# A graph layer with routed experts: a fifth buffer of messages and one-hot matrices, in room taken from the scratch of GpSimd's transfer descriptors

## The reference, cut to what matters

```
x = x + (segment_sum(layernorm(x)[src] * edge_weight, dst) @ W.T + b)
h = layernorm(x)
logits = h @ gate_w + gate_b;  idx = argmax(logits);  prb = softmax(logits)[idx]
pos = rank of the node in the queue of its expert;  kept = pos < capacity
y = (relu(h @ w1[idx] + b1[idx]) @ w2[idx] + b2[idx]) * prb * kept
x = x + y
```

## Time and profile before

| | us |
|---|---|
| median of 3 launches | 2920.89 (2913.4 to 2922.91) |
| the profiled launch, its own time | 2914.76 |
| its span, first to last instruction | 2912.8 |
| mean granted TensorE clock | 0.809 |

### The profile page before, as it was taken

How to read it: one execution, slowest core, us unless ns; L and a number is a source line. 1 busy time by engine, 2 the same in 40 slices (tenths; PEclk the granted TensorE clock), 3 DMA queues, 4 the chain that set the end, 5 groups by cost and what they waited for, 6 DMA issues and landing times.

```text
span 2912.8 us, 33576 instructions
## 1 busy us (share of the span) xinstructions
PE 1961.2 (67%) x9784; PEld 1260.8 (43%) x9784; DVE 1083.5 (37%) x5802; ACT 1086.4 (37%) x2562; POOL 1783.0 (61%) x1868
## 2 busy tenths in 40 slices
PE   2333355456888767777777777777777787785199
PEld 1111133234555544444444444444444454454088
DVE  7766233333444333333333333333343343333032
ACT  6666122223444433333333333333343343332033
POOL 6666666666666666666666666656666666655611
PEclk9999955667888887777777777778888888887599
DMA  6664333344434533443343444435444444433246
GB/s 218 192 202 152 94 94 100 100 131 130 152 116 150 161 118 96 131 145 108 100 143 109 130 126 126 130 94 163 131 131 133 128 130 158 161 118 129 88 158 234
DMA packets 139628, 394.12 MB, mean 135 GB/s; under 512 B 36117, under 2 KB 62741, under 8 KB 128806
## 3 DMA queue, kind: packets, MB, share of 16 engines
q0 software_dynamic: 89472, 243.63, 28.3%
q1 hardware_dynamic: 46276, 135.53, 13.4%
q10 hardware_dynamic: 3698, 12.80, 1.1%
HBM read 496.09 MB, written 40.76 MB: 184 GB/s over the span
## 4 chain that ended last, share of the span: by engine, by line
PE 33%; another core or an unknown queue 30%; DVE 13%; ACT 13%; issue 9%; DVEq 0%; DMA 0%; ACTq 0%; SPq 0%; POOL 0%; POOLq 0%
PE ps L1010 10%; PE ps L980 6%; PE ps L898 5%; PE ps L907 3%; PE ps L998 2%; ACT hmid L815 2%; PE ps L989 2%; ACT L791 2%; PE ps L938 2%; ACT L736 1%; ACT msg L770 1%; DVE aggT L1223 1%; ACT pairs L777 1%; ACT hmid L809 1%
## 5 line engine op out<-in xcount | busy, mean ns | idle before, releaser
L655 POOL DMA_INDIRECT msg<-normed,src_sb x1457 | 1387.7, 952 | 799.6 <-issue 389.8
L1010 PE MATMUL ps<-wsl,hmid 128*128 128x256 f32 x1680 | 488.0, 455 | 165.7 <-ACT hmid L815 123.3
L1223 DVE TENSOR_TENSOR aggT<-aggT,ps 128x192 f32 x293 | 103.9, 354 | 1315.1 <-remote 651.2
L1010 PEld LDWEIGHTS ps<-wsl,hmid 128*128 128x128 f32 x1680 | 383.7, 235 | 275.5 <-issue 200.6
L898 PE MATMUL ps<-msg,onehot 128*32 128x256 f32 x3322 | 445.8, 516 | 79.2 <-issue 48.0
L777 ACT COPY pairs<-ps 128x256 f32<-128x256 f32 x293 | 111.6, 381 | 882.6 <-remote 438.8
L907 PE MATMUL ps<-shift,pairs 128*128 128x96 f32 x1172 | 230.8, 328 | 226.9 <-ACT pairs L777 183.9
L980 PE MATMUL ps<-wsl,hTf 128*128 128x512 f32 x680 | 351.5, 665 | 3.0 <-ACT hTf L804 1.7
L815 ACT ACTIVATE hmid<-ps,wsl 128x128 f32<-128x128 f32 x840 | 230.9, 381 | 317.8 <-remote 210.0
L907 PEld LDWEIGHTS ps<-shift,pairs 128*128 128x128 f32 x1172 | 185.0, 224 | 291.7 <-ACT pairs L777 231.4
L655 POOL DMA_INDIRECT msg<-in_x,src_sb x204 | 196.2, 962 | 100.4 <-issue 56.8
(11 more groups left out here) (134 smaller groups left out, 2293.0 us busy)
## 6 DMA issues: line engine op xcount, KB each, us to landing
wsl<-in_wsecond SPq DMA_DIRECT2D x105, 1152.0 KB
wsl<-in_wfirst SPq DMA_DIRECT2D x105, 1028.0 KB
msg<-normed,src_sb POOLq DMA_INDIRECT x1457
xrow<-in_x SPq DMA_DIRECT2D x97, 128.0 KB
wsl<-in_x SPq DMA_DIRECT2D x24, 512.0 KB
normed<-wsl ACTq DMA_DIRECT2D x24, 512.0 KB
hin<-rows_by_expert SPq DMA_DIRECT2D x89, 130.0 KB
msg<-in_x,src_sb POOLq DMA_INDIRECT x204
```

Of the source, the lines that this page charges most:

```text
L655: pool.indirect_dma_start(out=msg[:, m + j, :], out_offset=None, in_=x if t < RAW else ln_dram, in_offset=bass.IndirectOffsetOnAxis(ap=src ...
L1010: last = nc.tensor.matmul(ps[:, Y, 0:D], hmid[:, c, :], w2_at(v % 2)[:, c, :], start=c == 0, stop=c == FC - 1)
L1223: dve.tensor_tensor(columns, columns, ps[:, t % 2, D:D + KD * TWIN].rearrange("p (k c) -> p k c", k=KD), ALU.add).then_inc(s_added, 1)
```

## The change

The ring gets a fifth slot: third t lies in slot t % 5, and POOL waits for the matmuls of third t - 5 before it fills it. `msg` grows by 6 KB and `onehot` by 768 bytes of a partition, and one more semaphore of each of `s_msg` and `s_mm` is made. The scratch for descriptors is 8,192 bytes instead of 16 KB. `POOL_LAG`, the three thirds by which VectorE makes one-hot matrices ahead, and the list of events stay.

```diff
-RING = 4
+RING = 5
...
-    nc = bacc.Bacc("TRN2", target_bir_lowering=False, num_devices=1)
+    nc = bacc.Bacc("TRN2", target_bir_lowering=False, num_devices=1, dynamic_dma_scratch_size=8192)
```

## The result

| | before | after |
|---|---|---|
| median, us (4 runs each) | 2921.9 (2913.4 to 2925.1) | 3008.0 (2997.1 to 3018.6) |
| ratio, 95% interval | | 1.0294 (1.0257 to 1.0330) |
| the profiled execution, us (its span) | 2914.8 (2912.8) | 3009.0 (3007.1) |

Slower by 2.9%: 2998 was forecast, the change against the median is +86 us against +77, and it is inside both ranges. But the experiments leave only part of the reason as it was given, and they show something that no row of the kernel before could: the hold on which all of it rests is there on some chips and not on others.

A forecast was written before the change was run, and what follows sets the result against it. The prediction took late slot releases to set the pace, PE's results being held while POOL issues without pause. Its terms, -3 + 70 + 10 = +77 us on 2914.8, gave 2992, and 6.1 for the median gave 2998; range 2868 to 3035.

The forecast's parts named there:

- the hold: Gather stretch and tail: behind some six to eight POOL transfers without a pause, PE's results come late until POOL pauses.
- rival A: Whole kernel at the same pace: full ring, depth worth nothing, node stays at 27.65 us; 2918 us, chance 22%.
- The fifth slot is worth nothing where the ring is full: POOL's ring waits: one third further ahead, same releases, gain per third 0; only the start's wait goes, -3 us.
- The scatter, +2.2 us a node: Nodes from 1100 us on: POOL waits at the scatter, then runs 13 transfers; the release moves by 2.2 us a node.
- The run one transfer (1.25 us) longer: POOL's long run at a node: 13 transfers instead of 12, one issue of 1.25 us more.
- The start is 0.9 us later: POOL's long run at a node: starts at 1528.05 instead of 1527.16, after waiting at the scatter for slot_i.
- How many nodes: Gather stretch: 32 nodes in 1100 to 1980 us, +70; about five of 23 after, +10; before 1100 us, 0.
- The scratch: Descriptor room halved: room is not what POOL waits for, so 0 us; upper bound +107.
- The tail: Last thirds and outputs: gathers end some 8 us earlier, but a scatter waits anyway; 0 us, bound -8.
- +70 and +10: Cost in us of the scatter's later release: +70 from 1100 to 1980 us, +10 from 1980 to 2618 us.
- B: Rival, ring waits: PE's lateness is its own, an extra slot rides over late releases; -60 us, 2861 us, chance 28%.
- C: Rival, descriptor scratch: less room makes each 40 transfers cost a drain of 2.3 us; +107, 3028 us, chance 6%.

The follow-up runs named there:

- the pauses: Kernel before, with POOL waiting before every fourth output until all outputs issued so far have landed: 2893.8 us against 2941.7, ratio 0.9819, on a slower chip.
- now + 5: Changed kernel with each node's scatter one third later in POOL's order (POOL_LAG 5, LAST_LAG 3): 3030.5 us, ratio 1.0291 to the kernel before.
- now + 7: Changed kernel with each node's scatter behind third now + 7 instead of now + 4: ratio to the kernel before 1.0007 on a faster chip, 1.0051 on a slower.
- the wait alone: Kernel before, four slots, with the scatter one third earlier (POOL_LAG 3 instead of 4), so POOL waits for slot_i: 2990.1 us against 2941.7, ratio 1.0154.
- now + 6: Kernel before, four slots, with each node's scatter behind third now + 6 instead of now + 4: ratios 0.9998 and 0.9988 on two faster chips.

## Why the prediction was right

*The hold.* Right on chips A, B and D, and in the tail tested by a change of its cause (the pauses, 44 matmuls in 100 us to 595 on one chip). In the gather stretch the distance from POOL's last issue to the release has the same median, 2.81 and 2.80 us, behind runs of 12 and of 13. The "six to eight transfers" behind which the prediction lets the hold set in stand in none of its rows. ScalarE's next rows in the run that starts at 1527.16:

```profile
1537.09 0.59 ACT L809 COPY hmid<-ps 128x512 f32<-128x512 f32 x1 [2.51 <-PE ps L980]
1539.22 0.59 ACT L809 COPY hmid<-ps 128x512 f32<-128x512 f32 x1 [1.54 <-remote]
1544.24 2.18 ACT L815 ACTIVATE hmid<-ps,wsl 128x128 f32<-128x128 f32 x8 [4.43 <-remote]
```

It still gets results during the eighth and the tenth transfer, and then none until the run is over.

The rule of the Trainium skill that was weighed against the hold (SBUF — State Buffer, "SBUF: two separate sides": PE waits for nobody) fits chips C and E, where PE had 694 matmuls beside 69 transfers and 689 beside 66 in 100 us, and not the others. (By it rival A would have held, which the prediction calls the second and lists first.) The cause of the hold is still open. That it comes from the chip, or from its state at that time, and not from the program is shown, as the same program takes 2414 and 2936 us.

*The fifth slot is worth nothing where the ring is full.* Right: POOL's 300 to 683 us are unchanged, and its ring waits before 683 us nearly so (82.4 us from "remote" and 12.8 at L898, before 89.8 and 5.1). The wait at 37.37 is gone, but the 3 us are not gained: third 38 starts 0.5 us later than before.

*The scatter, +2.2 us a node.* The size was nearly right (the pair of runs 27.21 to 29.03 us, +1.8; 59 us in 35 nodes where 70 in 32 stood), and one of the two parts of the mechanism in full. "The run one transfer (1.25 us) longer" is what the runs show: the long part grows by 1.21 us here, by 1.21 with now + 5, and by 1.15 between now + 7 and the change on chip D. "The start is 0.9 us later" by the wait at the scatter is measured at 0.61 here and 1.08 on chip D, where the sum of both parts, 2.2 us, is the one forecast. But with the wait gone (now + 5) the short part still grows, by 0.42 us, and a loss of 89 us stays; so not all of the later start is the wait's. How much is, is open: in the ring of four the wait alone made the short part 1.11 us longer and the long one 0.30 shorter. What was too narrow is the step "a place that does not move when the ring grows": I took the 13th transfer to follow from the scatter's fixed place and its wait, while the fifth slot gives 13 with the scatter one third later too, because the two thirds of 6 columns now stand in one run. With the scatter in the short run (now + 7) the long one comes back to 12.

*How many nodes.* The 10 us taken for thirds 227 to 290 were 27, still inside the bound of 51; eight runs of POOL have 13 transfers there, and none had before. The 14 nodes before third 122, for which 0 was taken, lost 8. Only one run has 13 there, so what they lost is not explained by it.

*The scratch.* 0 was taken, and it costs 8 us (0.26%) on a chip with the hold, with no gap that would show where. Whether tiles lie elsewhere with the smaller scratch was not looked at, so that its cause is open. On chip C five slots and the small scratch together cost 0.02%, which is no change by its interval. Part of the measured loss, some 8 of 86 us if chip A is like chip B, is therefore the scratch's and not the scatter's.

*The tail.* 0 was taken, -2 was measured.

The two terms that made the sum (+70 and +10) had the right sign; the -3 didn't come. The errors (+5, +8, -11, +17 and -2 us along the table's stretches, 17 us in all) partly cancelled, so that 2998 came within 10 us of the median is in part luck. Luck in the chip is in it too: on chip D the same change costs 122 us, and the forecast was +77.

*The rivals.* A (the same pace) is what happens on a chip without the hold, by what the five-slot variants showed there; the changed kernel itself was not run on one. B (POOL could ride over late releases) fell: the waits before 683 us stayed, and on a chip without the hold one or two of 289 releases are late, by 0.5 us or less, so PE is not late of its own accord there. C had the right sign, less than a tenth of the size (8 us of 107), and none of its gaps.

The best measured version on a chip with the hold is the kernel before with the pauses in its tail (0.982); on one without, none is more than 0.12% faster than the kernel before.

## What to carry to other kernels

A deeper ring also moves everything that has a fixed place in the producer's order; count what then stands in one uninterrupted run, and place the odd transfer in the shorter one. Where several engines that wait for different things are let go in the same moment, and that moment follows a third engine's pause, test it by adding a pause: it is two lines, and it showed here what moving waits couldn't. And time a close variant on more than one chip before believing in its mechanism: here one program had two bounds.

## What the runs showed of the hardware

- The same program takes 2414 and 2415 us on two chips and 2922, 2936 and 2942 us on the others (or 2922 and 2942 on one chip at two times: the chip of the result isn't known apart). POOL's issue is 0.95 + 0.30 us on both, and its busy time the same (1783.0 us on chip A, 1787.3 on chip C). What differs is its wait for the ring: 451 us in the earlier trace rows, 0.5 us on chip C with the scatters at now + 6.
- On the slower kind, PE does one matmul in 2.8 us in the tail while POOL issues in a row, 44 to 52 in 100 us beside 76 to 78 transfers; on the faster it does 694 beside 69.
- The matmuls' busy time, whose ends are modelled, is shorter too without the hold: the page has PE busy 1783.0 us on chip C and 1961.2 us in the earlier trace rows for the same 9784. The mean granted clock differs too, 0.865 against 0.809, and how much of the difference is the clock's was not separated.
- The loss by the same change was 86 us on chip A and 122 us on chip D.
- 8 KB of room for descriptors instead of 16 costs 0.26% (0.13 to 0.38) on a chip with the hold, without a gap between two gathers of a third.
